# A gated cross-attention layer: another order of the first operations of the program

## The reference, cut to what matters

```python
x = x + tanh(g_xattn) * xattn(layernorm(x), ctx)         # x: 2 x 1024 x 512, ctx: 2 x 2048 x 512
x = x + tanh(g_ffn) * int8_ffn(layernorm(x), rhs)

def layernorm(x):  return (x - mean(x)) / sqrt(var(x) + 1e-5)

def xattn(latents, context):
    lat = layernorm(latents) * ln_lat_g + ln_lat_b       # latents have been normed once already
    ctx = layernorm(context) * ln_ctx_g + ln_ctx_b
    q = lat @ Wq                                          # 512 x 1024, 16 heads of 64
    k, v = split(ctx @ Wkv)                               # 512 x 2048
    k = rope(k, cos, sin)
    p = softmax(clip(q @ k.T / 8, -11, 11))
    return (p @ v) @ Wo + bo
```

## Time and profile before

| | us |
|---|---|
| Median of 3 runs (1571.20 to 1574.33) | 1573.42 |
| The profiled execution, its own time | 1573.17 |
| Its span in the profile | 1571.3 |
| PE busy | 1493.8 (95%) |
| DVE busy | 1323.4 (84%) |
| ACT busy | 701.4 (45%) |
| POOL busy | 132.6 (8%) |

### The profile page before, as it was taken

The page is one execution under the profiler, slowest core; times in us unless marked ns, Lnnn a source line. Parts: engine busy times, 40 slices in busy tenths (PEclk is TensorE's granted clock), DMA queues, the critical chain, the costliest instruction groups (busy, mean ns, idle before and its releaser), DMA issues. The chain is left out here.

```text
span 1571.3 us, 22090 instructions
## 1 busy us (share of the span) xinstructions
PE 1493.8 (95%) x7888; PEld 868.4 (55%) x7896; DVE 1323.4 (84%) x1272; ACT 701.4 (45%) x778; POOL 132.6 (8%) x71
## 2 busy tenths in 40 slices
PE   3999999999998999999999999999999999998875
PEld 3788888888885344444444444444444444445553
DVE  7866667666746998999999999999999999997997
ACT  3442222222224555555555555555555555552221
POOL 2310000000001300000000000000000000005553
PEclk9999999999999999999999999999999999999998
DMA  5674565555587242253154044144234325105331
GB/s 191 243 255 169 172 190 161 189 158 168 165 241 221 80 122 69 68 135 98 50 121 121 27 121 121 45 103 121 66 82 126 77 65 135 41 28 134 128 113 53
DMA packets 121998, 195.30 MB, mean 124 GB/s; under 512 B 18368, under 2 KB 67520, under 8 KB 115808
## 3 DMA queue, kind: packets, MB, share of 16 engines
q1 hardware_dynamic: 119360, 190.49, 41.8%
q10 hardware_dynamic: 2592, 4.20, 0.7%
HBM read 114.70 MB, written 79.95 MB: 124 GB/s over the span
## 5 line engine op out<-in xcount | busy, mean ns | idle before, releaser
L932 ACT ACTIVATE prob<-score_ps 128x1024 f32<-128x1024 f32 x512 | 496.2, 1021 | 379.7 <-PE score_ps L861 379.5
L1016 DVE TENSOR_TENSOR prob_sum<-prob_sum,prob 128x2048 f32<-128x2048 f32 x224 | 515.9, 2303 | 0.5
L874 PE MATMUL value_ps<-prob,v_st 128*64 128x512 f32 x2048 | 497.4, 606 | 10.5 <-DVE prob L1022 10.1
L861 PE MATMUL score_ps<-q_st,k_st 64*128 64x512 f32 x3072 | 425.7, 409 | 2.5 <-PEq L102 2.1
L861 PEld LDWEIGHTS score_ps<-q_st,k_st 64*128 64x128 f32 x3072 | 268.7, 184 | 256.2 <-ACT prob L932 187.8
L1022 DVE TENSOR_SCALAR prob<-prob 128x2048 f32<-128x2048 f32 x256 | 313.8, 1226 | 68.1 <-ACT prob L932 64.2
L874 PEld LDWEIGHTS value_ps<-prob,v_st 128*64 128x64 f32 x2048 | 124.4, 136 | 250.5 <-issue 202.3
L645 DVE TENSOR_TENSOR k_cos<-k_raw,rope 128x1024 f32<-128x1024 f32 x32 | 39.2, 1225 | 99.9 <-ACT k_raw L546 99.9
L1305 POOL TENSOR_TENSOR o_lo<-o_in,o_hi 128x1024 fp32r<-128x1024 f32 x16 | 39.0, 2438 | 879.5 <-POOLq L115 872.6
L551 ACT ACTIVATE v_out<-proj_ps 128x1024 f32<-128x1024 f32 x31 | 32.0, 1031 | 136.6 <-PE proj_ps L228 136.6
L546 ACT ACTIVATE k_raw<-proj_ps 128x1024 f32<-128x1024 f32 x31 | 31.9, 1029 | 105.2 <-PE proj_ps L228 104.0
(11 more groups left out here) (118 smaller groups left out, 1294.1 us busy)
## 6 DMA issues: line engine op xcount, KB each, us to landing
k_st<-k_scr SPq DMA_DIRECT2D x128, 256.0 KB, 6.2
k_scr<-k_hi SPq DMA_DIRECT2D x64, 256.0 KB, 2.7
v_scr<-v_out SPq DMA_DIRECT2D x32, 512.0 KB, 3.5
k_scr<-k_lo SPq DMA_DIRECT2D x64, 256.0 KB, 3.9
q_st<-q_scr SPq DMA_DIRECT2D x16, 1024.0 KB, 10.3
v_st<-v_scr SPq DMA_DIRECT2D x16, 1024.0 KB, 13.2
q_scr<-q_hi SPq DMA_DIRECT2D x32, 256.0 KB, 3.6
q_scr<-q_lo SPq DMA_DIRECT2D x32, 256.0 KB, 3.7
```

Source lines behind the costliest of these rows:

```text
L861: last = pe.matmul(score_ps[:, half, a, :], k_st[slot][rows, k_part, s * P:(s + 1) * P], q_st[slot][rows, q_part, cols], start=(t == 0), s ...
L874: last = pe.matmul(value_ps[rows, cols], v_st[slot][:, s, rows], prob[:, s % PSLOT, a, cols], start=(s == 0), stop=(s == STEPS - 1))
L932: act.activation(prob[:, s % PSLOT, :, cols], score_ps[:, half, :, :], ACT.Exp, scale=SCALE).then_inc(exped, 1)
L1016: dve.tensor_tensor(total, total, prob[:, s % PSLOT, :, :], ALU.add).then_inc(added, 1)
```

## The change

It does six things.

1. One pass in place of two. For the chunks of x the root is taken of `(1 + EPS) * var + EPS * EPS` instead of `var + EPS`, with a new constant `eps_sq`. This is both norms in one: the second would divide by the root of `v / (v + EPS) + EPS`. All second passes go away.
2. The first chunk comes in four DMAs, one for each tile, and is measured, normed and transposed tile by tile (`SINGLE`, `turn_singles`).
3. wq is staged by halves of its columns instead of halves of its rows: `wq_hi` and `wq_lo` are now [128, 2, KT, 512]. Groups m = 0 to 3 read the first half alone, m = 4 to 7 the second. The DMAs are still 512 KB each, of runs of 2 KB in place of 4 KB.
4. The low parts of wq go from POOL to DVE (`wq_rest`), one before the split of the first chunk, one behind it. On ACT the affine step of the first chunk now stands before the split of the second half.
5. The tanh of the gates and the wait for their DMAs move from ACT's beginning to just before the last context chunk. There it shares a function table with the Exp that stood there before.
6. PE transposes the identity into bank 3 of `proj_ps` 56 times before the first chunk and 10 times behind it (`keep_busy`).

```diff
-    FRONT_TILES = 1
-    FRONT = (slice(0, FRONT_TILES), front_moments_made, ...)
-    BACK = (slice(FRONT_TILES, CT),) + CHUNK[1:]
+    SINGLE = [(slice(t, t + 1), front_moments_made, front_meanvar_made, front_std_made, front_rstd_made, front_normed)
+              for t in range(CT)]
+    WARM_EARLY = 56
+    WARM_LATE = 10
...
             if w < 2:
                 for k in range(2):
-                    row = (2 * w + k) * P
-                    sp.dma_start(w_stage[:, s, k * INNER:(k + 1) * INNER], wq[row:row + P, :]).then_inc(stage_in[s], 16)
+                    sp.dma_start(w_stage[:, s, k * INNER:(k + 1) * INNER].rearrange("p (t c) -> p t c", c=WQ_COLS),
+                                 wq[2 * k * P:(2 * k + 2) * P, w * WQ_COLS:(w + 1) * WQ_COLS]
+                                 .rearrange("(t p) c -> p t c", p=P)).then_inc(stage_in[s], 16)
...
-        for w in range(2):
-            pool.wait_ge(w_hi_made, w + 1)
-            pool.tensor_tensor(wq_lo[:, 2 * w:2 * w + 2, :], w_stage[:, w, :], ...)
...
+            act.activation(std[:, tiles], meanvar[:, tiles, 1], ACT.Sqrt, bias=(eps_sq if twice else eps_col)[:, 0:1],
+                           scale=1.0 + EPS if twice else 1.0).then_inc(std_made, 1)
...
-        act.wait_ge(gates_in, 32)
-        act.activation(gate_tanh[:, :], gates[:, :], ACT.Tanh)
-        act.wait_ge(consts_set, 4)
+        act.wait_ge(consts_set, 5)
         act.activation(warm[:, 0:1], eps_col[:, :], ACT.Sqrt)
-        sqrt(0, FRONT)
-        sqrt(0, BACK)
+        for part in SINGLE:
+            sqrt(0, part)
         split_weight(0)
-        sqrt(1, FRONT)
-        sqrt(1, BACK)
-        split_weight(1)
         act.wait_ge(gains_in, 16)
         affine(0)
+        split_weight(1)
...
-                if m == 0 and n + 1 < QCH:
-                    measure(n + 1, slot, passes(n + 1)[1], True)
-                if m == 1 and n + 1 < QCH:
-                    normalise(slot, passes(n + 1)[1])
...
+        def keep_busy(times):
+            for i in range(times):
+                pe.transpose(proj_ps[:, 3, 0:P], ident[:, :], ident[:, :])
+
+        def turn_singles():
+            for t in range(CT):
+                pe.wait_ge(front_normed, t + 1)
+                for k in range(KT):
+                    last = pe.transpose(turn_ps[:, k, t * P:(t + 1) * P], raw[:, 0, t, k * P:(k + 1) * P], ident[:, :])
+                    if t == CT - 1:
+                        last.then_inc(turned, 1)
+
         pe.wait_ge(ident_set, 2)
-        turn(0, 0)
-        pe.wait_ge(w_hi_made, 2)
+        keep_busy(WARM_EARLY)
+        turn_singles()
+        keep_busy(WARM_LATE)
```

More of the change, by code:

```diff
@@ L240, in projections @@
     spacer = sb("spacer", [P, 1])
+    eps_sq = sb("eps_sq", [P, 1])
     warm = sb("warm", [P, 2])
@@ L276, in projections @@
     wkv_lo_made = sem("wkv_lo_made")
-    front_in = sem("front_in")
+    front_in = [sem(f"front_in{i}") for i in range(CT)]
     moments_made = sem("moments_made")
@@ L319, in banks, with turns_before @@
         return acc[:, first_bank:first_bank + 2, :]
[L321 to L326, removed]
+    def turns_before(n, part):
+        return part[0].start if part is not CHUNK else n - 1
     def slot_read(eng, n):
@@ L382, in chunk_rows @@
             return x[n * CH:(n + 1) * CH, :] if n < QCH else context[(n - QCH) * CH:(n - QCH + 1) * CH, :]
[L384 to L387, removed]
+        for t in range(CT):
+            sp.dma_start(raw[:, 0, t, :], x[t * P:(t + 1) * P, :]).then_inc(front_in[t], 16)
         sp.dma_start(gains[:, :, :], affines).then_inc(gains_in, 16)
@@ L483, in split_weight, with sqrt @@
             act.wait_ge(stage_in[s], 32 * (w // WST + 1))
-            dst = wq_hi[:, 2 * w:2 * w + 2, :] if w < 2 else wkv_hi[:, w - 2, :]
+            dst = wq_hi[:, w, :, :] if w < 2 else wkv_hi[:, w - 2, :]
             act.activation(dst, w_stage[:, s, :], ACT.Copy).then_inc(w_hi_made, 1)
-        def sqrt(p, part=CHUNK):
+        def sqrt(n, part=CHUNK):
             tiles, _, meanvar_made, std_made, _, _ = part
-            act.wait_ge(meanvar_made, p + 1)
-            act.activation(std[:, tiles], meanvar[:, tiles, 1], ACT.Sqrt, bias=eps_col[:, 0:1]).then_inc(std_made, 1)
+            twice = isinstance(n, int) and n < QCH
+            act.wait_ge(meanvar_made, turns_before(n, part) + 1)
+            act.activation(std[:, tiles], meanvar[:, tiles, 1], ACT.Sqrt, bias=(eps_sq if twice else eps_col)[:, 0:1],
+                           scale=1.0 + EPS if twice else 1.0).then_inc(std_made, 1)
         def affine(n):
@@ L522, in _ @@
                 if (n, m) == (0, 0):
-                    sqrt(2)
-                if m == 1 and n + 1 < QCH:
-                    sqrt(passes(n + 1)[1])
+                    sqrt(1)
                 if m == 6 and n + 2 <= QCH:
-                    sqrt(passes(n + 2)[0])
+                    sqrt(n + 2)
                 if m == (4 if n == 0 else 3):
@@ L534, in context_chunk @@
             if ahead:
-                sqrt(last_pass(c + QCH + 1))
+                sqrt(c + QCH + 1)
             for what, j in order:
@@ L558, in _ @@
                 context_chunk(2 * i + 2 - slot, slot, True)
+        act.wait_ge(gates_in, 32)
+        act.activation(gate_tanh[:, :], gates[:, :], ACT.Tanh)
         act.activation(warm[:, 1:2], eps_col[:, :], ACT.Exp)
@@ L563, in _, with measure @@
     def _(dve):
[L564 to L570, removed]
+        def measure(n, slot, part=CHUNK):
+            tiles, moments_made, meanvar_made, _, _, _ = part
+            if part is CHUNK:
+                dve.wait_ge(raw_in[slot], 16 * (n // 2 + slot))
             else:
-                dve.wait_ge(raw_in[slot], 16 * chunk_turn(n))
+                dve.wait_ge(front_in[tiles.start], 16)
             for t in range(CT)[tiles]:
@@ L605, in tok_split, with wq_rest @@
                               ALU.subtract).then_inc(tok_lo_made, 1)
[L607 to L611, removed]
+        def wq_rest(w):
+            dve.wait_ge(w_hi_made, w + 1)
+            dve.tensor_tensor(wq_lo[:, w, :, :], w_stage[:, w, :].rearrange("p (t c) -> p t c", c=WQ_COLS),
+                              wq_hi[:, w, :, :].bitcast(F32), ALU.subtract).then_inc(w_lo_made, 1)
+        for i, part in enumerate(SINGLE):
+            measure(0, 0, part)
+            if i:
+                normalise(0, 0, SINGLE[i - 1])
+        normalise(0, 0, SINGLE[-1])
+        wq_rest(0)
         tok_split(0, 0)
-        measure(1, 1, 2, False)
+        wq_rest(1)
+        measure(1, 1)
         for n in range(QCH):
@@ L673, in turn @@
         def turn(n, slot):
[L675 to L682, removed]
+            pe.wait_ge(normed, n)
             for k in range(KT):
-                if not isinstance(n, int) or n >= 1:
-                    pe.wait_ge(affine_made, KT * (n - 1) + k + 1)
-                for t in range(FRONT_TILES if parted else 0, CT):
+                pe.wait_ge(affine_made, KT * (n - 1) + k + 1)
+                for t in range(CT):
                     last = pe.transpose(turn_ps[:, k, t * P:(t + 1) * P], raw[:, slot, t, k * P:(k + 1) * P],
```

39 lines of the change are left out of this document (18 added, 21 removed).

## The result

| | before | changed |
|---|---|---|
| Median of 6 runs | 1572.34 us | 1557.78 us |
| Lowest and highest | 1571.20 to 1577.12 | 1557.32 to 1559.98 |
| Profiled execution | 1573.17 | 1557.32 |
| Its span | 1571.3 | 1555.5 |

The ratio is 0.9906, with a 95% interval of 0.9891 to 0.9921. The forecast was 1559.0 us, 1.2 above the median, in a range of 1556.0 to 1563.5. The gain between the medians is 14.6 us, and between the two profiled executions 15.85.

What follows compares the result with a forecast made beforehand. PE was taken as the bound, its queue full from the first matmul at 28.14 us except one hole. Gains of 11.5 us at the beginning and 2.75 at chunk 2 made 14.2 off 1573.17: 1559.0 us, range 1556.0 to 1563.5.

Steps and rivals of the forecast that it cites:

- DMAs: First-chunk loads: tile 0 at 4.71 us, tiles 1 and 2 about 6.4 and 7.4, last 8.13; wq's first half 10.8.
- DVE over the tiles: First chunk: measuring (0.92 us a tile) and norming (0.72) interleaved on DVE, the last tile normed at 12.05 us.
- ACT and DVE to the first matmul: Beginning: wq split from 10.95, affine 12.9 to 15.7, low part to 15.2, casts to 16.6, first matmul 16.65 us.
- POOL beside DVE: Kernel before, first chunk: three norming operations read as taking 5.73 us beside a POOL operation of 4.50.
- The dummies: 66 identity transposes around the first chunk's: clock rises after 3.5 us, early 56 end at 10.0, no cost on the path.
- The clock at the first group: First q group: PE idle 3 us loses the full clock, so second group at 21.1 instead of 32.62, 11.5 us gained.
- a clock that stays up: Rival at the first q group: full clock holds, 12.8 us gained there, total 1557.6 us; chance 0.24.
- The second hole: PE's wait before chunk 2's transposes disappears with the second pass, 2.75 us gained.
- Other removed passes: Second passes in chunks 1 and 3, 5 us of DVE each, lay beside PE's work without a wait: 0.
- Never rises: Rival at the beginning: identity transposes never raise the clock, gain 10.0 us, total 1563.2 us; chance 0.14.
- in series: Rival at the beginning: each identity transpose must end before the next, 0.42 us each, total 1575.7 us; chance 0.04.
- hole stays: Rival at chunk 2: PE's wait stays in part or whole, up to 2.75 us back, 1561.8 us; chance 0.08.

Runs made afterwards that it cites:

- low parts on POOL: Changed kernel with wq's low parts computed on POOL again instead of DVE; median 1566.34 us against 1557.78.
- 32 late dummies: Changed kernel with 32 identity transposes in place of 10 behind the first chunk's real transposes; median 1557.46 us against 1557.78.
- wq by rows: Changed kernel with wq staged by halves of its rows again, every q group waiting for both halves; median 1562.44 us against 1557.78.
- no late dummies: Changed kernel without the 10 identity transposes behind the first chunk's real ones, the 56 early ones kept; median 1559.89 us against 1557.78.
- 100 early dummies: Changed kernel with 100 identity transposes in place of 56 before the first chunk; median 1561.96 us against 1557.78.
- tanh first: Changed kernel with the wait for the gates and the tanh at ACT's beginning again; median 1558.85 us against 1557.78.
- one pass alone: Kernel before the change with only the second passes dropped and the root of the folded variance taken; median 1564.47 us against 1572.34.

## Why the prediction was right, and where not

*What bounds the kernel.* Right: PE's queue is full behind the second group, and 12.8 + 2.8 us reached the attention stage whole.

*DMAs.* Tile 1 landed at 6.77, not 6.4, tile 0 at 4.95; it had no effect. The first half of wq was there when ACT asked at 10.95.

*DVE over the tiles.* 11.87 measured, 12.05 forecast. The terms of the earlier trace rows carried over: DVE had only two waits for a DMA.

*ACT and DVE to the first matmul.* Split at 10.95, affine at 12.86 to 15.65, casts to 16.40, first matmul at 16.55; the forecast had 10.95, 12.9 to 15.7, 16.6, 16.65. The times are right, one reading beside them is not: the forecast charged DVE's low part with 2.29 us on the path, though its own two chains end together. The second cast started 0.06 us after the affine step, so the low part cost at most about 0.1.

*POOL beside DVE.* The forecast read the 5.73 us of three norming operations as one stretch. By the trace the first of them took 4.81, up to 22.50, just past the end of POOL's operation at 22.22, and the other two the usual 0.5 each. The sum doesn't rest on it, but the expected price of low parts on POOL came out too small for want of it.

*The dummies.* Half right. They were covered as forecast, by DVE's chain and ACT's split, and they raise the clock, but it rose after 6 us, not 3.5. They lasted 9.22 us in place of 7.9 (8.02 with 32 late dummies, so 7.9 was within what other executions show), and so the real transposes came later and the late dummies ended at 14.17, not 13.7.

*The clock at the first group: the step that failed.* I had PE idle for 3 us and took the fall. The idle time was 2.37, and the clock held: second group at 19.81, not 21.1. The term was 12.8, not 11.5, which is the rival of a clock that stays up, 1557.6. The size of the fall was off too: it was taken as 4.48 us for the group, from a group whose last four matmuls ran fast. Where it ran at the slow clock in part or whole, it took 4.3 to 5.3 us (wq by rows aside, which has a wait inside the group). The rule that I drew from two rows (held after 2.75, lost after 3.34) is not a rule. In the experiments' profiles the first group took 3.3 us after 2.34, 2.37 and 1.12 us of idle time, but 4.4 after 2.35, 4.4 after 2.72, and 4.3 after 3.25. Much the same gap was survived twice and lost once. In four of these profiles (no late dummies, 100 early dummies, tanh first, wq by rows) the granted clock fell 0.3 to 0.8 us after PE was at work again, so the length of the gap alone doesn't settle it. That the total still came within 1.2 us is in part luck: this term could have gone either way.

*The second hole.* Right in place, size and cause: it is gone with the second pass and comes back with it, 2.8 us.

*Other removed passes, the tanh's new place, later stages.* All 0, as forecast: 1081.3 us against 1081.5.

*The sum.* 14.2 us forecast, 15.85 between the profiled executions: 1.3 more from the first group, where the clock held; 0.2 in the later stages; the rest is rounding. Between the medians it is 14.6, since six runs put the kernel before at 1572.34 and not at the 1573.42 from which the forecast started.

*The rivals.* "Never rises" fell to the dummies' own records, "in series" to the distance between them (56 in 9.22 us), "hole stays" to PE's waits.

## What to carry to other kernels

Where one engine is busy to the end, find the point from which its queue never runs empty. The time to that point is worth its full length, and it can be costed link by link from durations in the trace of before; in ten profiles the rest of the stage took the same time within 0.3 us. When an elementwise operation moves between GpSimd and VectorE, price what it holds up rather than its own length: two operations of about 4.7 us on POOL cost 6.4 us at the first matmul here and 1.9 more of clock, while the first of them on DVE, 2.3 us long, lay beside ACT's affine step and cost at most about 0.1. After changing the order of work, look at when each buffer comes free, which loads the DMA queue starts then, and which small transfers stand behind them.

## What the runs showed of the hardware

- A cast or a norming on DVE that runs beside an elementwise operation of POOL can be held until that one has ended; in these rows one of them got through for each POOL operation. Casts of 128x1024, 0.69 us each alone, took 3.78 and 4.98 beside two POOL operations of 4.51 and 4.95, and ended about 0.55 us after them; in the kernel with one pass alone two casts took 6.12; in the kernel before a norming operation of 0.55 took 4.81 beside one of 4.50.
- Transposes raise TensorE's clock from 1.2 to 2.4 GHz: 421 to 272 ns for one, about 6 us after the first in the changed kernel, sooner in others.
- The clock can be lost around an idle time of 2.35 us (100 early dummies) and kept after 2.37 (changed kernel). It can fall after PE is at work again: at about 21.7 us with 100 early dummies, where the first matmul started at 21.30. What decides these runs don't show.
- The stages behind the start of the attention stage took 1078.0 to 1082.7 us over these profiles, with the same work. Which part of it is the clock in the output stage's gaps stays open.
